# Relational message passes of a four-layer graph network: ring of eight gathered groups, one-hot tiles three pairs ahead, block products a turn later; splits and projection in parts

## What is computed

```python
edge_index = stack([src, dst])
h = maximum(_layernorm(x), 0);  x = x + L0(h)   # two SAGE convolutions, batch norm between them
h = maximum(_layernorm(x), 0);  x = x + L1(h)   # two relational hops
h = maximum(_layernorm(x), 0);  x = x + L2(h)   # GIN: h + neighbours, two dense layers, batch norm
h = maximum(_layernorm(x), 0);  x = x + L3(h)   # attention over 5 node anchors and 5 edge anchors

def _rgcn_layer(h, src, dst, et, W, root_w, b, N):      # one relational hop
    xw = einsum('ni,rio->rno', h, W)
    cnt = zeros((R, N)).at[et, dst].add(1.0)
    msg = xw[et, src] / cnt[et, dst][:, None]
    return segment_sum(msg, dst, N) + h @ root_w + b
# L1: twice  h = _rgcn_layer(out, ...); h = maximum(h, 0) in the first; out = 0.5*out + 0.5*h
```

## Time and profile before

| | us |
|---|---|
| median of 3 runs | 5902.55 (5898.19 to 5908.68) |
| the profiled execution, its own time | 5876.22 |
| its span | 5874.4 |
| pass 0 / pass 1 | 1206.2 / 1196.0 |
| PE busy | 3488.4 (59% of the span) |
| DVE busy | 2356.2 (40%) |
| POOL busy | 2236.6 (38%) |
| ACT busy | 1354.9 (23%) |

### The profile page before, as it was taken

One profiled execution on the slowest core, in us unless ns is written; L12 is line 12 of the kernel. 1 busy time (PEld: TensorE's weight loads), 2 busy tenths in 40 slices (PEclk: granted clock), 3 DMA queues, 4 the chain that ended last, 5 costly groups with the idle time before them and its releaser, 6 DMA issues.

```text
span 5874.4 us, 68831 instructions
## 1 busy us (share of the span) xinstructions
PE 3488.4 (59%) x18857; PEld 2341.4 (40%) x18858; DVE 2356.2 (40%) x6119; ACT 1354.9 (23%) x2986; POOL 2236.6 (38%) x2337
## 2 busy tenths in 40 slices
PE   5599997998633333333333333337994566655566
PEld 3255553444332222222333233333443455544455
DVE  7756566113322222222122222223116555555556
ACT  2555451001200000000000000001002555555555
POOL 3000000000366666665666666660001444444442
PEclk8699998998756666666555555558995777777777
DMA  2111113222522222222111111113220221212122
GB/s 70 52 68 46 67 45 129 94 87 87 160 56 67 69 67 67 70 66 68 46 45 46 46 46 46 46 45 115 108 87 17 44 45 43 45 41 41 43 50 53
DMA packets 264711, 371.64 MB, mean 63 GB/s; under 512 B 63252, under 2 KB 200251, under 8 KB 256299
## 3 DMA queue, kind: packets, MB, share of 16 engines
q1 hardware_dynamic: 186790, 251.51, 12.9%
q0 software_dynamic: 74464, 114.31, 8.7%
q10 hardware_dynamic: 3364, 4.69, 0.3%
HBM read 261.10 MB, written 109.21 MB: 63 GB/s over the span
## 4 chain that ended last, share of the span: by engine, by line
PE 21%; issue 18%; POOL 16%; another core or an unknown queue 9%; DVE 5%; DMA 2%; DVEq 2%; ACT 2%; ACTq 0%; POOLq 0%; SPq 0%
POOL GS L716 16%; PE psum L1296 7%; PE psum L1437 5%; PE psum L1242 3%; DMA GS<-xw_table,stage 2%; PE psum L1464 2%; DVEq L1779 1%; DVE GS L1779 1%; PE psum L1389 1%; PE psum L1390 1%; PE psum L1431 1%; PE psum L1221 1%; DVEq L1786 0%; ACT O L1056 0%
## 5 line engine op out<-in xcount | busy, mean ns | idle before, releaser
L716 POOL DMA_INDIRECT GS<-xw_table,stage x1664 | 1576.7, 948 | 2277.3 <-issue 1925.9
L1296 PE MATMUL psum<-HA,HT 128*128 128x512 fp8e4 (+1 forms) x5733 | 1253.7, 369 | 63.8 <-DVE HT L1962 63.8
L1242 PE MATMUL psum<-GS 128*128 128x96 f32 x3328 | 691.1, 382 | 712.7 <-DMA GS<-xw_table,stage 611.1
L716 POOL DMA_INDIRECT HA<-p_table,stage x624 | 603.3, 967 | 1213.6 <-DMA p_table<-HT 536.6
L1242 PEld LDWEIGHTS psum<-GS 128*128 128x128 f32 x3328 | 634.5, 287 | 765.7 <-issue 762.2
L1296 PEld LDWEIGHTS psum<-HA,HT 128*128 128x128 bf16 x5733 | 554.5, 100 | 642.8 <-DVE HT L1962 64.8
L1779 DVE TENSOR_SCALAR GS<-iota,HT,wt 128x96 f32<-128x96 f32 x1680 | 473.7, 349 | 449.8 <-issue 448.2
L1793 DVE TENSOR_TENSOR HA<-HA,psum 128x96 f32 x208 | 52.8, 254 | 1358.7 <-remote 859.4
L1221 PE MATMUL psum<-Wcat,HT 128*128 128x512 f32 x196 | 177.6, 1060 | 476.7 <-DVE HT L2255 443.4
L991 ACT ACTIVATE HA<-psum 128x392 fp8e4<-128x392 f32 x784 | 349.5, 494 | 345.5 <-PE psum L1201 332.3
L1201 PE MATMUL psum<-edge_cols 128*128 128x196 bf16 x1568 | 341.0, 351 | 39.1 <-ACT HA L991 23.6
(11 more groups left out here) (363 smaller groups left out, 4179.0 us busy)
## 6 DMA issues: line engine op xcount, KB each, us to landing
HT<-dst_rows SPq DMA_DIRECT2D x212, 256.0 KB
xw_table<-HT SPq DMA_DIRECT2D x100, 512.0 KB, 3.2
HA<-adj SPq DMA_DIRECT2D x26, 1600.0 KB, 6.3
adj<-HA SPq DMA_DIRECT2D x13, 3136.0 KB, 9.5
HA<-adj SPq DMA_DIRECT2D x26, 1536.0 KB, 9.7
GS<-xw_table,stage POOLq DMA_INDIRECT x1664
HA<-p_table,stage POOLq DMA_INDIRECT x624
h_table<-HA SPq DMA_DIRECT2D x4, 960.0 KB, 5.7
```

The source lines that it names most:

```text
L716: nc.gpsimd.indirect_dma_start(out=to, out_offset=None, in_=table, in_offset=bass.IndirectOffsetOnAxis(ap=idx, axis=0)).then_inc(done, 16)
L1242: last = nc.tensor.matmul(bank[h][:, 0:WINDOW], G3[g][:, j, :], S_pair[h][:, t, :], start=(t == 0), stop=(t == 2 * GT - 1))
L1296: last = nc.tensor.matmul(bank[s][:, 0:w], Hs4[:, b, t, :], adj_tile[s][:, b * GW:b * GW + w], start=(b == 0 and t == 0), stop=(b == SRCS ...
```

## The change

**In the passes.** The ring becomes eight groups (the four old places and four in H), with eight semaphores `gathered`; CREDIT is 8, so POOL waits for the sum of eight groups back. ACT stages indices when the gathers of two iterations back have landed instead of when their sums are done. The one-hot tiles have four places (in T), three pairs ahead. The sums have four PSUM places. The combine trails by 6 iterations, the products by 7, with two places `hop_sum`; in ACT's program the evacuation of iteration it stands between the stagings, and SP stores one block later.

**Beside them.** `normalise_and_split` interleaves ACT's 20 normalised blocks with the split before SAGE 1 and GIN; the split before SAGE 2 starts on the first half of H. In the batch norm between the SAGE convolutions POOL does the second half; in the last one POOL does 18 of 50 blocks. The clearing of O moves from POOL to DVE, behind the split. The last layer norm is made in two parts (28 and 22 blocks, DVE 12 of each, ACT the rest); the projection goes in 13 steps of four blocks, transposed straight from H, and its results are copied by ACT; DVE adds H to X in one instruction. Some semaphores of the preparation are merged.

```diff
-LAG = 5
+LAG = 6
+PRODUCT_LAG = 7
+AHEAD = 3
-CREDIT = 4
+CREDIT = 8
-        S_pair = [S[:, i * 2 * GT * WINDOW:(i + 1) * 2 * GT * WINDOW].rearrange("p (j d) -> p j d", d=WINDOW) for i in range(2)]
+        S_pair = [T[:, 2048 + i * 2 * GT * WINDOW:2048 + (i + 1) * 2 * GT * WINDOW].rearrange("p (j d) -> p j d", d=WINDOW) for i in range(4)]
+        ring = G3 + [H[:, g * GT * P:(g + 1) * GT * P].rearrange("p (j f) -> p j f", f=P) for g in range(4)]
+        hop_sum = [tail[:, 1024:1024 + P], H[:, 4 * GT * P:4 * GT * P + P]]
+        pair_sums = [bank[i][:, 0:WINDOW] for i in (0, 1, 5, 7)]
...
-                                gather(G3[g][:, j, 0:P], table, stage16[u][:, t:t + 1], gathered[g])
+                                gather(ring[u * 4 + g][:, j, 0:P], table, stage16[u][:, t:t + 1], gathered[u * 4 + g])
...
-            def stage_columns(l, it, u):
+            def stage_columns(l, it, u, round_before=None):
                 if not is_block(it, 0, 1):
-                    act.wait_ge(windows_summed, GROUPS * l + it * 4)
+                    for g in range(4):
+                        act.wait_ge(gathered[u * 4 + g], 64 * (ITERS // 2 * l + round_before))
...
-                    if l == 0 and not is_block(it, *range(LAG)):
-                        evacuate_next(it - LAG)
+                    if l == 0 and not is_block(it, *range(PRODUCT_LAG)):
+                        evacuate_next(it - PRODUCT_LAG)
...
                 pe.wait_ge(combined, b + 1)
-                pe.wait_ge(hop_evac_d, b + 1)
+                pe.wait_ge(hop_evac_d, b + 2)
...
+                    windows(k + AHEAD, (q + AHEAD) % 4)
+                    dve.wait_ge(windows_summed, GROUPS * l + 2 * k + 2 + CREDIT)
+                    dve.wait_ge(sums_added, PAIRS * l + k + 4)
...
+                    if h == 0 and combining:
+                        combine(i2 * 2 + u - LAG, u)
+                    if h == 1 and u in with_evacuation:
+                        evacuate(i2 * 2 + u - PRODUCT_LAG, 1 - u)
...
+            late_half = slice(NB // 2, NB)
+            nc.gpsimd.tensor_tensor(H3[:, late_half, :], O3[:, late_half, :], in_late_half(sd[:, :]), ALU.mult).then_inc(bn_scaled, 1)
+            nc.gpsimd.tensor_tensor(H3[:, late_half, :], H3[:, late_half, :], in_late_half(mu[:, :]), ALU.add).then_inc(h_ready, 1)
...
-            pool.wait_ge(combined, 2 * HOP_BLOCKS)
-            nc.gpsimd.memset(O[:, :], 0.0).then_inc(rest_cleared, 1)
+            nc.gpsimd.tensor_tensor(T3[:, BY_POOL, :], T3[:, BY_POOL, :], in_blocks(sd[:, :]), ALU.mult).then_inc(bn_scaled, 1)
+            nc.gpsimd.tensor_tensor(X3[:, BY_POOL, :], X3[:, BY_POOL, :], T3[:, BY_POOL, :], ALU.add).then_inc(bn_scaled, 1)
...
+            normalise_part(*NORM_PARTS[0])
+            dve.wait_ge(bn_scaled, 5)
+            normalise_part(*NORM_PARTS[1])
```

More of the change, by code:

```diff
@@ L900, in turn_own, with split @@
+            def split(q, first, ready):
+                act.wait_ge(h_first, first)
+                high(0)
+                high(1)
+                middle(q, 0)
+                act.wait_ge(h_ready, ready)
+                for c in range(2, 5):
+                    high(c)
+                    middle(q, c - 1)
+                middle(q, 4)
             def turn_own(q, roots):
@@ L1255, in rest_pass @@
+                with pe.Fori(0, PRODUCT_LAG // 2) as i2:
+                    iterations(i2, ())
+                iterations(PRODUCT_LAG // 2, (1,))
+                with pe.Fori(PRODUCT_LAG // 2 + 1, ITERS // 2) as i2:
+                    iterations(i2, (0, 1))
+                for b in range(PRODUCTS_IN_PASS, HOP_BLOCKS):
+                    of_block(b, b % 2)
             def rest_pass(z):
@@ L1802, in sum_pass @@
+                with dve.Fori(0, LAG // 2) as i2:
+                    iterations(i2, (), combining=False)
+                iterations(LAG // 2, (1,))
+                with dve.Fori(LAG // 2 + 1, ITERS // 2) as i2:
+                    iterations(i2, (0, 1))
+                dve.wait_ge(sums_added, PAIRS * (l + 1) + 4)
                 for b in range(IN_PASS, HOP_BLOCKS):
-                    for step in beside:
-                        step(b)
+                    combine(b, b % 2)
+                    evacuate(b - 1, (b - 1) % 2)
```

381 lines of the change are left out of this document (232 added, 149 removed).

## The result

The changed kernel takes 5888.16 us (median of 20 runs, 5875.52 to 5917.62), the kernel before on the same chip 5911.69 us (5887.11 to 5918.23): **ratio 0.9973, interval 0.9964 to 0.9982**, 24 us less. Forecast were 5823 us, 79 us less, and a range up to 5885. The sign was right, the size was not, and the time lies outside the range. (The forecast started from 5902.55 us, the median of three runs; with all 20 the kernel before stands 9 us higher, so the starting point explains 9 of the 65 us between forecast and measurement.)

The account below looks back on a forecast made before the run. POOL was taken to set the pace, losing time in pauses paid once per run of gathers. Passes -57, tails +11.6 and side edits -34 made -79, from 5902.55 to 5823 us; range 5570 to 5885.

Parts of the forecast that it names:

- the price of a pause: Pass 1: POOL's pause after runs of 40 to 44 gathers taken as 5.5 us beyond the gap, 42 us less.
- rival B: Passes: each gather leaves a debt, so half as many pauses are twice as long; only sides and tails count, 5880; chance 0.10.
- Pass 0: First relational pass: one pause per 32 gathers, 26 in all, 5.8 us each, 15 us less.
- D: Pass 0: pauses also hold combine, product and evacuation, 6.5 us more in each of 26, +169, 5992; chance 0.04.
- Tail: After pass 0: four trailing block products instead of two, 4.3 us each, +8.6 us.
- GIN's start: Before GIN's first matmul: split interleaved with ACT's normalisations, clearing moved off POOL, -8; +3 for pass 1's longer tail.
- The first layer's -3: Start of the first layer: same interleaving of normalisation and split, half of the 5.5 us counted, -3.
- The batch norm on POOL: Before the second layer: two of four 3.49 us DVE instructions go to POOL, taken at -1.
- GIN's end: From GIN's end to the attention: POOL takes 18 of 50 blocks, projection starts after 28, gain 21 to 26, taken -22.
- A: Passes: the ring hides the pauses altogether and POOL never waits, about 5570; chance 0.15.
- C: Passes: DVE's one-hot tiles stay late all the time and DVE becomes the bound, +156, 6036; chance 0.08.
- E: Another semaphore holds POOL at 16 gathers and POOL's arithmetic loses the split's gain by contention, 5890 to 5914; chance 0.03.

Follow-up runs that it names:

- e3: The changed kernel, but POOL waits for the group four back instead of eight, so at most 16 gathers are in flight; 5847.96 us, ratio 0.9962.
- e15: The changed kernel with only two of each pair's eight one-hot tiles built and multiplied, all gathers kept, on a chip with pauses; 5808.73 us, ratio 0.9896.
- e10: The changed kernel itself, beside the kernel before, on the chip without pauses; 5118.92 us, ratio 0.9983.
- e7: The changed kernel with the old passes and both batch norms on DVE alone, other outside edits kept, on the chip without pauses; 5099.06 us, ratio 0.9947.
- e1: The changed kernel with the relational passes as before (ring of four), all edits outside them kept; 5843.86 us, ratio 0.9944.
- e16: The changed kernel with the old passes and both batch norms on DVE alone, other outside edits kept, on a chip with pauses; 5842.73 us, ratio 0.9955.
- e14: The changed kernel with eight more sequencer instructions on PE per pair, on a chip with pauses; 5874.10 us, ratio 0.9997.

## Why the prediction was wrong

**The step that failed** is the price of a pause: "I take 5.5, nearer to the flat end, since the step from 24 to 28 is smaller than the one before". Over the gap the pauses after 32 gathers of pass 0 are 7.5 us in the mean of 18, not 4.6 + 1.2. In pass 1 runs of 40 did not come about: after 32 gathers the mean is 5.9 us (12 pauses), and between them stand short runs of 4 gathers with 3.9 us (9 pauses). A single pause there does not keep the quotient, but neighbours together do: a run of 28 with 1.1 us and the run of 4 behind it with 4.9 come to 6.0 us for 32. Over a whole pass the loss is 0.22 and 0.19 us per gather, about the number that stood in rival B, to which I gave 0.10 and 5880 us. The rows had it: 3.2 us at 16 and 4.5 at 24 are 0.20 and 0.19 per gather, and 5.0 at 28 is 0.18. I read a curve into three points of two passes where one quotient explained them. (B's total, 22 us less than before, is nearly the measured 24, but in part by luck: it left out the 15 us more of pass 0.)

**Bottleneck.** That POOL's idle time sets the passes was right, and the floor of 1040 us was confirmed by the chip where POOL never pauses. That the pauses are the whole excess holds, their count did not: I took 52 and 34.7 equal ones, the trace of before has 53 and 41 of mixed lengths. That a pause is "a price of the visible progress, paid once per run" was wrong: e3 pays the same with short runs, e15 with very long ones.

**Pass 0.** One pause per 32 came as forecast. The term that failed is its length: 5.8 us were taken, 7.5 measured. It is not the chain of D: the block's product ran from 2430.89 and was done at 2435.06, before the pause began, and in the pause only ACT's two instructions from 2446.81 and the staging stand ahead of POOL, about the 1.2 us that I had counted. The loss rose by 18 us, where 15 us less was forecast. With the ring held at four (e3) it fell by 6 us against before, so in these executions the ring alone accounts for 24.

**Tail.** Forecast +8.6, measured +14.0. Two more products give 9.5 (e10 against e7). The rest is backlog: 36 matmul records of pass 0 start after its last gather, where before there were 16 and e3, with the short ring, has 12, and 31.1 us instead of 39.7.

**Side edits.** GIN's start, -5 with its tail, came to -4.0, but by luck: without the longer tail (e1) it is -4.8 where -8 was forecast, so the longer tail costs about 1 us where +3 was forecast, and the two misses cancel. The first layer's -3 did not last: PE's first matmul there starts at 232.67 instead of 237.67, but the first batch norm begins at 966.57 instead of 966.23. The batch norm on POOL was taken at -1 and costs 5.2: PE's start at 991.20 against 985.96 (against e16's 984.40 it is 6.8). That is what follows if the two engines exclude each other. The Trainium skill (SBUF — State Buffer, Who interferes with whom) says just that of a DVE instruction with two SBUF inputs beside a GpSimd one that reads SBUF, and here the trace agrees, 10.09 us against 3.49. I had the rule and split the difference. GIN's end gave 14.0, not 22. The term that was too small is DVE's share, forecast at 8.9 us and measured at 18.5 (9.31 + 9.14; all of it on DVE alone took 7.02 + 6.83 in the earlier trace rows). A wait that I had not seen came with it: in ACT's program the second root stands behind the copies of the first blocks' products, so DVE waits 7.16 us before 4515.47. Together they are more than the 8 us that are missing; which later term was too large, no run shows.

**The other rivals.** A (no pauses) is what a chip without them shows, but with the old ring too, so it is no merit of the ring. C did not happen: DVE's tiles come late, but POOL waits in long pauses, and pass 1 did not get longer. E was wrong in that nothing holds POOL at 16 gathers (runs of 32 came about), and right in that the arithmetic on POOL loses by contention.

**What stays open.** Shown is that on some chips POOL loses 0.16 to 0.24 us per gather, whatever the ring (e3), the number of PE's instructions (e14) or with a quarter of the tiles (e15), and that late in a run the other engines' instructions come slowly. What in the chip does this, and why one chip is free of it, no run shows. Whether lengthened gathers pay the same debt as pauses, or DVE's instructions make a part of the debt, was tested by no run alone.

Two things in the traces narrow it. It is not the loading of instructions: in 1560 to 2600 us the changed kernel loads as little with pauses (the first two rows) as without (e10, the last two).

```profile
q8 instruction: 2, 0.03, 0.0%
q14 instruction: 2, 0.02, 0.0%
...
q8 instruction: 2, 0.03, 0.0%
q14 instruction: 3, 0.02, 0.0%
```

And the traces themselves differ between the chips. In the two passes of e10 the trace holds 27408 landings of DMAs, some 16 per gather; for the same kernel, on the chip of the profile after, it holds 3821. Before the passes, where few gathers run, the two have 2880 and 2385. So where POOL pauses, far fewer landings are on record, in just the stages with the gathers. Either both come from one cause, or the recording of so many events itself holds the engines up; the second is a rival that nothing here tests, since every time in this document is that of a recorded execution. It also makes the releasers named on such chips ("issue", "remote") less certain than on the other.

## What to carry to other kernels

When a producer pauses periodically, divide each pause by the length of the run before it, before reasoning on buffers: if the quotient is constant, a deeper ring only makes fewer and longer pauses, and one run with the ring cut short by a single wait constant shows it. Longer trails have their own bill at the end of a pass (9.5 us for two more products). And before arithmetic is moved to POOL beside DVE's, it should be priced with the two taking turns: here both batch norms were slower than on DVE alone (24.6 us against 18.2 to PE's start in the first, 18.5 against 13.7 in the last).

## What was not expected of the hardware

One chip of the four that ran the experiments runs the same program in 5126 us, where the other three and the first session take 5872 to 5912. In the two passes the difference is 1206.2 + 1196.0 against 2079.4 us (e7), 323 us, nearly all of it POOL's pauses (its loss is 168 and 159 us in the one case, 4 and 4 in the other). In the attention, 624 gathers, it is 1349.2 against 934.2 us from the first gather on, 415 us, and there POOL waits for others: 502 us for ACT's staging before, 93 in e7. A change that is judged on one kind of chip should be judged on the other too.
